# Combining the two experts' halves inside the tile loop instead of in a last stage

## What is computed

```python
x = x + _layernorm(_L0_attn_ref(_layernorm(x), ...))          # gated linear attention
x = x + _layernorm(_L0_ffn_ref(_layernorm(x), ...))           # mixture of experts

def _L0_ffn_ref(x, router_w, router_b, gate_w, up_w, down_w):
    logits = jnp.einsum('bth,eh->bte', x, router_w) + router_b   # 8 experts
    topv, topi = jax.lax.top_k(logits, 2)
    gates = jax.nn.softmax(topv, axis=-1)
    # for each expert e: w = gate of e in this row, or 0
    h = jax.nn.silu(x @ gate_w[e].T) * (x @ up_w[e].T)           # 512 wide
    out = out + (h @ down_w[e].T) * w[..., None]

def _layernorm(x, axis=-1, eps=1e-05):
    m = jnp.mean(x, axis=axis, keepdims=True)
    v = jnp.var(x, axis=axis, keepdims=True)
    return (x - m) / jnp.sqrt(v + eps)
```

## Time and profile before

| | us |
|---|---|
| median of 3 runs | 1332.94 |
| lowest and highest | 1332.85, 1337.09 |
| the profiled execution | 1333.82 |
| its span, first to last instruction | 1332.0 |
| PE busy | 1240.2 (93%) |
| DVE, ACT, POOL busy | 789.2, 674.4, 552.0 |
| chain that ended last, PE's share | 65% |

### The profile page before, as it was taken

One profiled execution on the slowest core, in us unless ns is written; L12 is line 12 of the kernel. 1 busy time (PEld: TensorE's weight loads), 2 busy tenths in 40 slices (PEclk: granted clock), 3 DMA queues, 4 the chain that ended last, 5 costly groups with the idle time before them and its releaser, 6 DMA issues.

```text
span 1332.0 us, 27589 instructions
## 1 busy us (share of the span) xinstructions
PE 1240.2 (93%) x8008; PEld 1037.8 (78%) x8008; DVE 789.2 (59%) x2374; ACT 674.4 (51%) x1717; POOL 552.0 (41%) x674
## 2 busy tenths in 40 slices
PE   3999999999999999999999999939999999999975
PEld 1778788787787787887877877828899999988952
DVE  2667767767777777677677777643333333333327
ACT  2466565475465665654754656423444444443426
POOL 2223534535436446355354364142333333333326
PEclk9999999999999999999999999969999999999998
DMA  7000100101101001001011010033311111111164
GB/s 274 9 17 9 41 14 26 32 13 34 32 8 40 21 18 40 12 28 32 12 36 32 8 32 16 21 141 106 104 48 48 51 49 48 49 46 44 48 229 178
DMA packets 60282, 67.99 MB, mean 51 GB/s; under 512 B 7488, under 2 KB 50144, under 8 KB 59872
## 3 DMA queue, kind: packets, MB, share of 16 engines
q1 hardware_dynamic: 50656, 46.03, 10.8%
q0 software_dynamic: 8448, 17.45, 4.0%
q10 hardware_dynamic: 1152, 4.19, 1.1%
HBM read 38.50 MB, written 29.15 MB: 51 GB/s over the span
## 4 chain that ended last, share of the span: by engine, by line
PE 65%; DVE 13%; issue 8%; DMA 4%; ACT 4%; POOL 3%; DVEq 1%; SPq 0%; POOLq 0%; ACTq 0%
PE pO L723 8%; PE pA L560 8%; PE pO L576 8%; PE pO L578 6%; PE pW L605 4%; PE pA L714 4%; PE pA L715 4%; PE pJ L714 4%; PE pJ L715 4%; PE pT L588 3%; PE pJ L494 2%; PE pJ L605 2%; DVE S_raw L1076 2%; PE pA L542 2%; DMA expert_out<-y,tail 2%
## 5 line engine op out<-in xcount | busy, mean ns | idle before, releaser
L1524 POOL DMA_INDIRECT expert_out<-y,tail x136 | 130.1, 957 | 264.1 <-ACT y L985 236.9
L576 PE MATMUL pO<-vJ,aT 128*128 128x128 f32 x1024 | 194.1, 279 | 0.0
L578 PE MATMUL pO<-S_mid,qT 128*128 128x128 f32 x896 | 173.2, 275 | 0.0
L840 ACT ACTIVATE sq<-pO 128x512 f32<-128x512 f32 x128 | 75.8, 592 | 184.8 <-PE pO L576 142.2
L576 PEld LDWEIGHTS pO<-vJ,aT 128*128 128x128 f32 x1024 | 153.8, 192 | 14.6 <-issue 13.2
L1099 DVE TENSOR_REDUCE ss<-sq 128x8 f32<-128x512 f32 x128 | 86.5, 676 | 100.6 <-ACT sq L840 100.6
L1458 POOL DMA_INDIRECT expert_rows<-x1n,rowi x120 | 117.1, 976 | 64.9 <-issue 39.5
L578 PEld LDWEIGHTS pO<-S_mid,qT 128*128 128x128 f32 x896 | 136.1, 192 | 0.0
L560 PE MATMUL pA<-qT,kT 128*128 128x256 f32 x512 | 133.3, 383 | 2.5 <-DVE qT L1060 2.5
L723 PE MATMUL pO<-wdown_sb,vJ 128*128 128x128 f32 x1088 | 132.7, 275 | 0.0
L723 PEld LDWEIGHTS pO<-wdown_sb,vJ 128*128 128x128 f32 x1088 | 126.8, 192 | 0.0
(11 more groups left out here) (225 smaller groups left out, 2604.0 us busy)
## 6 DMA issues: line engine op xcount, KB each, us to landing
xt<-expert_rows SPq DMA_DIRECT2D x69, 130.0 KB, 2.2
xa<-x SPq DMA_DIRECT2D x16, 256.0 KB, 2.8
xr<-x SPq DMA_DIRECT2D x16, 256.0 KB, 2.8
after_attention<-x SPq DMA_DIRECT2D x16, 256.0 KB, 2.4
arena<-after_attention ACTq DMA_DIRECT2D x8, 512.0 KB, 3.6
expert_rows<-zeros SPq DMA_DIRECT2D x8, 390.0 KB, 3.1
expert_out<-y,tail POOLq DMA_INDIRECT x136, 2.2
wgate_sb<-wgate SPq DMA_DIRECT2D x1, 2048.0 KB, 9.3
```

What stands on the lines that cost most here:

```text
L576: last = mm(o, aT[:, c % 2, p, h * P:(h + 1) * P], vJ[:, c, p, :], start=True, stop=(c == 0))
L578: last = mm(o, qT[:, p, c, 2 * h:2 * h + 2, :].rearrange("p r c -> p (r c)"), S_mid[:, c, p, :], start=False, stop=True)
L1524: g.indirect_dma_start(out=ys_dram, in_=y[:, k, :], in_offset=None, out_offset=bass.IndirectOffsetOnAxis(ap=tail[:, k, 1:2].bitcast(U32), ...
```

## The change

The expert stage does all, and nothing follows it. A row of `expert_rows` grows to 259 words: the 128 numbers, the gate, `PART` (the place in `expert_out` of the row's other half), `GOAL` (its place in the output) and x1 itself. y is no longer scattered but stored in order by SP (`save`), to the tile's own place in `expert_out`. POOL gathers, for each row of the tile, the other half (`partner`). If this expert is the row's earlier one, PART and GOAL are made to lie out of bounds (`early`), and the gather and the scatter skip the row; so a row is finished only in the tile of its later expert, where its other half has been stored already. Rows that are skipped are computed like all others, and come to nothing. `expert_out` is filled with zeros by SP during attention (`clear`).

In DVE's `tile(t, m, n)` tile t is multiplied, the partner of tile m = t-1 is added to y (`add_partner`) and statistics are taken, and tile n = t-2 is normalised and gets its x1. The reciprocal root is worked out on DVE from a first guess by bits and three Newton steps, which stand between the multiplies of tile t. POOL gathers for tile t and then scatters tile t-2 to the output (`move`). SP loads x1 and GOAL of a tile late (`load_late`) and PART and GATE early (`load_tail`). It takes each tile's address from a table `trow_i`, which DVE makes when the counts are known, so there is one loop for all experts.

In attention, x1 is copied by DMA into the rows (`x1_to_rows`) in place of the store to DRAM; `places` has two more instructions for PART; the pads are stored one sequence earlier, with 10 rows per partition in place of 6, and the scatter before the last ones waits for them.

```diff
-XW = HID + 2
+GATE, PART, GOAL, X1 = HID, HID + 1, HID + 2, HID + 3
+XW = X1 + HID
 @block.sync
-            for e in range(E):
-                with sp.Fori(0 if e == 0 else ends[e - 1], ends[e]) as t:
-                    load_tile(e, t)
...
+            with sp.Fori(0, rest + 1) as n:
+                load_rows(n + 3)
+                load_tail(n + 2)
+                save(n + 1)
+                load_late(n)
 @block.scalar
-                act.wait_ge(y_free, FIRST + t)
+                act.wait_ge(y_saved, FIRST + t * 16)
+                act.wait_ge(total_ready, FIRST + t * 2)
                 act.wait_ge(tail_kept, FIRST + t + 1)
 @block.vector
+            def keep_tail(t):
+                if not at_start(t):
+                    for k in range(2):
+                        dve.wait_ge(partner_in[k], t * 16)
+                dve.wait_ge(y_ready, FIRST + t * 2)
+                dve.wait_ge(meta_in, t * 16 + 16)
                 v.tensor_copy(tail[:].bitcast(U32), tail_next[:].bitcast(U32)).then_inc(tail_kept, 1)
+            def add_partner(t):
+                dve.wait_ge(y_ready, FIRST + t * 2 + 2)
+                for k in range(2):
+                    dve.wait_ge(partner_in[k], t * 16 + 16)
+                    if not at_start(t):
+                        dve.wait_ge(f_norm, t * 2 - 1 + k)
+                    v.tensor_tensor(total_y[:, k, :], y[:, k, :], partner[:, k, :], ALU.add)\
+                        .then_inc(total_ready, 1)
...
+            def normalise(t):
+                dve.wait_ge(f_guess, (t + 1) * (NEWTON + 1))
+                if not at_start(t):
+                    dve.wait_ge(done_out, t * 32)
+                for k in range(2):
+                    v.tensor_scalar(done[:, k, :], total_y[:, k, :], fmv[:, k, 0:1], frs[:, NEWTON, k:k + 1],
+                                    ALU.subtract, ALU.mult).then_inc(f_norm, 1)
...
+            def tile(t, m, n):
+                multiply(t, 0)
+                    half_var(n)
+                    halve_bits(n)
+                multiply(t, 1)
+                    first_guess(n)
+                    residue(n, 0)
+                multiply(t, 2)
+                    better_guess(n, 0)
+                    residue(n, 1)
+                multiply(t, 3)
+                    better_guess(n, 1)
+                keep_tail(t)
+                    residue(n, 2)
+                    better_guess(n, 2)
+                    normalise(n)
+                    keep_goal(n)
+                    add_partner(m)
+                    add_x1(n)
+                    row_stats(m)
+                    row_aggr(m)
 @block.gpsimd
-                    g.indirect_dma_start(
-                        out=ys_dram, in_=y[:, k, :], in_offset=None,
-                        out_offset=bass.IndirectOffsetOnAxis(ap=tail[:, k, 1:2].bitcast(U32), axis=0))\
-                        .then_inc(y_out, 16)
-                pool.wait_ge(y_out, t * 32 + 32)
-                pool.sem_inc(y_free, 1)
+            def gather(t, k):
+                if k == 0:
+                    pool.wait_ge(tail_kept, FIRST + t + 1)
+                    pool.wait_ge(y_saved, FIRST + t * 16)
+                pool.wait_ge(total_ready, t * 2 + k if not at_start(t) else FIRST)
+                g.indirect_dma_start(
+                    out=partner[:, k, :], in_=ys_dram, out_offset=None,
+                    in_offset=bass.IndirectOffsetOnAxis(ap=tail[:, k, 1:2].bitcast(U32), axis=0),
+                    bounds_check=E * CAP - 1, oob_is_err=False).then_inc(partner_in[k], 16)
+            def hand_out(t, k):
+                if k == 0:
+                    pool.wait_ge(done_ready, FIRST + t + 1)
+                    pool.wait_ge(goal_kept, t + 1)
+                g.indirect_dma_start(
+                    out=ov, in_=done[:, k, :], in_offset=None,
+                    out_offset=bass.IndirectOffsetOnAxis(ap=goal_i[:, k, :], axis=0),
+                    bounds_check=T - 1, oob_is_err=False).then_inc(done_out, 16)
...
+            with pool.Fori(0, rest) as n:
+                move(n + 3, n + 1)
```

More of the change, by code:

```diff
@@ L68, in build @@
     TILES = 2 * T // ROWS + E
[L69 removed]
+    assert TILES == TILES_MOST
     ctx = ExitStack()
@@ L431, in load_tile, with load_tail @@
+            def load_tail(t):
+                first = first_of(t, E * CAP - ROWS)
+                sp.wait_ge(tail_kept, FIRST + t)
                 settle(sp)
-                if e == 0:
-                    load_rows(t * ROWS)
-                else:
-                    load_rows(nc.s_assert_within(
-                        (t - ends[e - 1]) * ROWS + e * CAP, min_val=e * CAP, max_val=(e + 1) * CAP - ROWS,
-                        skip_runtime_bounds_check_because="tile t of expert e lies in its own rows"))
@@ L449, in _ @@
             settle(sp)
-            ysum = ys_dram[0:2 * T].rearrange("(k p n m) h -> k n p (m h)", k=2, p=P, m=TJ)
-            ob = out.rearrange("s l h -> (s l) h").rearrange("(p n m) h -> n p (m h)", p=P, m=TJ)
-            sp.wait_ge(y_out, ends[E - 2] * 32)
+            sp.wait_ge(done_out, rest * 32 + 96)
             settle(sp)
-            for n in range(TC):
-                sp.dma_start(ya[n], ysum[0, n]).then_inc(a_in[n], 16)
-            sp.wait_ge(y_out, total * 32)
-            settle(sp)
@@ new lines, in row_stats, with row_aggr, half_var @@
+            def row_stats(t):
+                dve.wait_ge(total_ready, FIRST + t * 2 + 2)
+                settle(dve)
+                for k in range(2):
+                    v.bn_stats(fst[:, k, :], total_y[:, k, :]).then_inc(f_stat, 1)
+            def row_aggr(t):
+                dve.wait_ge(f_stat, t * 2 + 2)
+                settle(dve)
+                for k in range(2):
+                    v.bn_aggr(fmv[:, k, :], fst[:, k, :]).then_inc(f_aggr, 1)
+            def half_var(t):
+                dve.wait_ge(f_aggr, t * 2 + 2)
+                v.tensor_scalar(fve[:], fmv[:, :, 1], LN_EPS, None, ALU.add).then_inc(f_var, 1)
+                v.tensor_scalar(fvh[:], fmv[:, :, 1], LN_EPS, -0.5, ALU.add, ALU.mult).then_inc(f_var, 1)
@@ new lines, in finish @@
+            def finish(t):
+                half_var(t)
+                halve_bits(t)
+                first_guess(t)
+                for r in range(NEWTON):
+                    residue(t, r)
+                    better_guess(t, r)
+                normalise(t)
+                keep_goal(t)
+            tile(0, None, None)
+            tile(1, 0, None)
+            tile(2, 1, 0)
+            with dve.Fori(0, rest) as n:
+                tile(n + 3, n + 2, n + 1)
+            finish(rest + 1)
@@ L1555, in _ @@
-            pool.wait_ge(x1_back, 16 * TC)
-            settle(pool)
-            offsets(0)
-            for n in range(TC - 1):
-                offsets(n + 1)
-                residuals(n)
+            g.memset(partner[:], 0.0).then_inc(partner_zero, 1)
+            pool.wait_ge(ys_zero, 16 * S)
+            settle(pool)
+            pool.wait_ge(partner_zero, 1)
+            settle(pool)
+            pool.wait_ge(counts_ready, 2)
+            rest = pool.value_load(rest_i[0:1, 0:1], min_val=E - 3, max_val=TILES - 3)
@@ L1564, with move @@
+            def move(t, n):
+                if t is not None:
+                    for k in range(2):
+                        gather(t, k)
+                if n is not None:
+                    for k in range(2):
+                        hand_out(n, k)
+            move(0, None)
+            move(1, None)
+            move(2, 0)
+            with pool.Fori(0, rest) as n:
+                move(n + 3, n + 1)
+            move(None, rest + 1)
+            move(None, rest + 2)
 def kernel(**inputs):
```

419 lines of the change are left out of this document (209 added, 210 removed).

## The result

The changed kernel takes 1475.53 us (median of 4, 1474.02 to 1476.57), the kernel before 1333.66 beside it: 1.1057 times as long (95% interval 1.1035 to 1.108), 142 us more. The profiled execution took 1476.57 with a span of 1474.7.

A forecast was written before the change was run, and what follows sets the result against it. The prediction took a DVE-POOL chain through DMA landings as the bound: tile 2's gather at 920.0, 65 laps of 7.9 (513.5) and drain 17.8 give span 1451.3; with 1.8 around it, 1453 us, range 1405 to 1531.

The forecast's parts named there:

- The ring (Part 3): Expert stage: closed chain DVE add, POOL gathers and scatters, landing, normalise, next add sets each tile's time; chance 0.80.
- The lap: One tile's turn of that chain: wake 0.79, three pitches 3.79, landing 2.39, DVE 0.96; taken as 7.9 us.
- The issues: POOL's indirect DMAs in the expert stage: pitch 1.26 us as before, despite bounds checks and skipped rows.
- the first rival: Expert stage: skipped rows make POOL's issues short, so DVE and PE set 5.7 us a tile; 1309 us, chance 0.06.
- The start (Part 5): Attention and start of expert stage: extra work mostly hidden, +1.0 us, bounds -3 and +12.
- The drain: After the last tile's gather: remaining issues, landings, normalisations and adds to the end of the span, 17.8 us.
- DVE's work (Part 2): DVE's instructions per tile in the expert stage: 5.8 us, from 5.2 to 7.0.
- SP (Part 4): SP's four row-number loads and four DMAs per tile: 4.9 us, hidden under 7.9.
- The bounds of the lap (Part 3): Limits for one tile's turn of the chain: 7.2 to 9.1 us, giving 1407 to 1531 us.
- PE as the bound: Expert stage: PE still sets the time, 5.46 us a tile; 1293 us, chance 0.01.
- TensorE's clock: Expert stage: idle PE drops to 1.2 GHz, mean 9.4 us a tile; 1551 us, chance 0.05.
- The fourth rival: Expert stage: DVE's second add and that of x1 delay the first gather, 0.7 us a lap; 1499 us, chance 0.08.

The follow-up runs named there:

- swap: The changed kernel with POOL issuing the two scatters of tile t-1 before the two gathers of tile t+1: 1650.38 us, 1.1976 times the kernel before.
- open2: The changed kernel with two buffers for done and goal_i, and the store of y issued by ACT, not SP: 1454.97 us, 1.0904 times the kernel before.
- newton1_b: The changed kernel with one Newton step in place of three, on a chip with slow SP steps: 1548.98 us, 1.1301 times the kernel before.
- two_done: The changed kernel with two buffers each for done and goal_i: 1570.88 us, 1.1412 times the kernel before; repeated, 1541.42 us, 1.1229 times.
- before_clear: The kernel before plus only the change's 16 zero fills, into a DRAM tensor that nothing reads: 1333.16 us, 0.9996 times the kernel before.
- after_again: The changed kernel unaltered, run again as a control on a chip with slow SP steps: 1551.62 us, 1.1318 times the kernel before.
- lean2: The changed kernel with more second buffers, ACT storing y between silus, one SP row number less, two Newton steps: 1302.91 us, 0.9765 times the kernel before.
- two_all_b: The changed kernel with two buffers for done, goal_i, tail, partner and y, on a chip with slow SP steps: 1474.76 us, 1.0753 times the kernel before.

## Why the prediction was right, point by point

It gave 1453 us, 1405 to 1531, slower with 0.92; 1475.5 was measured, 22 above.

- **The ring (Part 3).** Right in its path, order and releasers. swap moved the lap nearly as forecast, to 10.05. Two buffers for `done` removed the wait of L1400, but not the 1.1 us a lap that were expected of it: 8.62 beside 8.71 on a chip on which SP was late, 7.79 in open2. DVE's waits in every tile, and newton1_b, show that DVE's work was no bound. On the first chip two_done alone was never run; open2 stands for it there, and held a third ring of nearly the same length, which the prediction did not see. It does not appear in the changed kernel's time, since the first ring is longer.
- **The lap.** Predicted 7.9, measured 8.08. The sizes: wake 0.79, measured 0.91; three pitches 3.79, measured 3.99; landing until DVE goes on 2.39, measured 2.26; DVE 0.96, measured 0.88. In sum 8.04 in place of 7.93; rounding to 7.9 and a few longer laps give the rest. 65 laps cost 525.2 in place of 513.5: 11.7 of the 22 us.
- **The issues.** With a bounds check and half the rows skipped, they take 1.01 us (median of 136, L1634 and L1646; the longest 1.05) in place of the 0.958 of the earlier trace rows. No run has one of the two without the other, but together they do not shorten an issue, which was the point by which the first rival was to be decided.
- **The start (Part 5).** +1.0 predicted, +9.45 measured, inside the bound of +12: the term that failed, and by over 5 us, the prediction's own sign that Part 5 is wrong. Of its reasons for "hidden", the zeros were rightly costed at nothing (before_clear); the others together were not nothing.
- **The gather of tile 2** came at 928.30 in place of 920.0, all of it the late start.
- **The drain.** 17.8 predicted, 1474.7 - 1453.45 = 21.25 measured. Up to the start of the last scatter 15.8 (predicted 15.2). The last issue started at 1469.28 and the span ended 5.4 later, predicted 2.6. See below.
- **DVE's work (Part 2).** 5.8, and 5.82 where nothing held it up.
- **SP (Part 4).** "Hidden" held on the first chip, where SP waits for y in each tile. SP waits about 2.2 us of each lap there (115.1 in 53), so its loop takes about 5.9, not 4.9. On the chip of after_again the laps were 8.71 and SP nearly never waited. The price came from eight pad stores on a chip without the slow steps, and could not show them.
- **Luck in the chip.** On that other chip the changed kernel took 1551.6 us, above the range's 1531 (its ratio of 1.1318 is within it). The forecast knew nothing of chips that differ.
- **The bounds of the lap (Part 3).** 7.2 and 9.1 are not worked out alike. A landing of 2.0 counted until DVE goes on, as 2.8 is in the 9.1, gives 0.79 + 3.3 + 2.0 + 0.86 = 6.95. Nothing hung on it.
- **The rivals.** PE as the bound came true only in lean2. TensorE's clock: granted 0.97 in the stage, so it stayed at the upper level of 2.4 GHz but for short falls, although PE is busy in only 0.84 of it. The adds that hold up the gathers are told next.
- **The adds.** In the changed kernel they cost at most 0.12 a lap: the first gather starts 0.91 after the first add's end in place of 0.79, at 1203.03, when the add of x1 has been over since 1202.65, and its issue takes 1.04. But where the buffers let a gather start beside the adds, the price can be there. Timeline of two_all_b, DVE and POOL:

```profile
1189.07 0.49 DVE L1364 TENSOR_TENSOR total_y<-y,partner 128x128 f32<-128x128 f32 x2
1189.12 1.68 POOL L1650 DMA_INDIRECT partner<-expert_out,tail  x1 [1.46 <-issue]
1189.47 0.42 DVE L1422 TENSOR_TENSOR done<-done,late 128x256 f32<-128x256 f32 x1
...
1191.10 1.01 POOL L1650 DMA_INDIRECT partner<-expert_out,tail  x1 [0.30 <-issue]
```

  The gather that starts when the first add has begun takes 0.67 longer than the next. Which of them starts first matters. Another gather of the same trace had begun 0.08 before the first add, and no issue there that starts 0.05 or more before the adds beside it takes over 1.05:

```profile
1012.91 1.01 POOL L1650 DMA_INDIRECT partner<-expert_out,tail  x1 [0.30 <-issue]
1012.99 0.49 DVE L1364 TENSOR_TENSOR total_y<-y,partner 128x128 f32<-128x128 f32 x2
```

  The fourth rival had its mechanism and its price (0.7) about right and its place wrong: its gather waits for the add itself. By the rule of the Trainium skill that was weighed there (SBUF — State Buffer, section "SBUF: two separate sides"), a DVE instruction with two SBUF inputs and a GpSimd instruction that reads SBUF lock each other out, and the one that starts first goes first. The issue reads its row numbers from `tail`. The first pair of rows agrees, with 0.67 us. The second agrees for the issue, but the adds, begun later, were not held up (0.49 for the two, as at 1189.07). The prediction said that no row of before shows an add of two SBUF inputs beside an issue. One does: the add at 878.70 in the earlier trace rows ran within this issue, and neither was longer than usual:

```profile
878.09 0.95 POOL L1458 DMA_INDIRECT expert_rows<-x1n,rowi  x1 [0.30 <-issue]
```

Together: 11.7 (laps) + 8.3 (start, up to the gather of tile 2) + 3.4 (drain) = 23.4 on the span, 1451.3 + 23.4 = 1474.7.

## What to carry to other kernels

When a DMA's landing frees a single buffer on an engine that works in order, list every closed path through it and price each: with one buffer the lap is the sum of wake, issues, landing and what stands between, whatever the engines' shares. Opening the longest ring shows the next; here the first took 8.04 us, the third 7.8 in open2, and the second 6.9 by the expectation's sum, which no run showed alone. What brought PE back as the bound was more buffers together with an order that puts DMA issues and register loads where the engine waits anyway. A queue's own instructions have a price too, and one chip's price need not hold on another.

## What the runs showed of the hardware

- **A queue's plain instructions can become slow beside POOL's issues, on some chips.** Several of SP's steps per tile took 0.7 us each in place of 0.02 to 0.4, most of them while POOL issued indirect DMAs back to back, on two of the chips seen here, and not on the others. The laps of the changed kernel, in which SP was then late, were 41 us longer in sum. The cause was not found.
- **A chip can be 3% slower on the same program**: 1372.2 and 1375.7 against 1333.7. The changed kernel's attention ended 34 us later there. A ratio from one chip says little of another: 1.1057 and 1.1318 for the same two kernels.
- **The end of the program came over 3 us after the last landing.** The last scatter started at 1469.28, a landing takes 2.2, and the span ended at 1474.7. The last pieces of the chain are POOL's own:

```profile
1467.99 0.98 POOL out L1646
1468.98 1.29 POOLq L73
```

In the view of waits of SP's queue, 1440 to 1475, SP has seen the last landing and waits at the end of the block (L73):

```profile
SPq L73 <- PEq L73: 3.2, 1, 3.2
```

Whether the indirect DMAs cause this no run tells.

- **An indirect issue that starts just after DVE's adds from SBUF have begun is mostly longer**: up to 1.73 us in place of 1.01 in two_all_b, and 1.66 in lean2, where it costs PE nothing. One that starts 0.08 before the adds is not (1.01 at 1012.91).
- **A gather's landing takes longer than a scatter's**: the copy into `tail`, released by the gathers, started at 1207.33, 2.96 after the second gather's start at 1204.37, against 2.26 for the scatters. Both have 128 rows of 512 bytes with half of them skipped. In the changed kernel two more issues follow the gathers; in swap, where none does, it was still 2.74 (1209.20 to 1211.94).
